# First loads on one queue in order of need, and the second group's patch products spread out, in a fusion block with routed experts

## The reference

```python
tokens = jnp.einsum('bpi,hi->bph', patches, W) + b
h = concatenate([cls, tokens], 1) * pos_embed
h = concatenate([h, txt], 1)                       # 16 x 193 x 128

x = layernorm(h)                                   # attention, 8 heads of 16
qk = x @ Wqk + bqk
q, k = elu(qk[..., :c]) + 1, elu(qk[..., c:]) + 1
z = 1 / (einsum('bhnd,bhd->bhn', q, mean(k)) + 1e-6)
kv = einsum('bhnd,bhne->bhde', rope(k) * scale, x * scale)
out = einsum('bhnd,bhde->bhne', rope(q), kv) * z
h = h + out + depthwise_conv3(x)                   # the "taps"

x = layernorm(h)                                   # 8 experts, best 2 of each token, and a shared one
shared = (silu(x @ sw1) * (x @ sw3)) @ sw2
y_e = (silu(x @ w1[e]) * (x @ w3[e])) @ w2[e]
h = h + sum over the best two of p_e * y_e + shared
```

## Time and profile before

| | us |
|---|---|
| median of three runs | 264.31 |
| the profiled execution's own time | 264.31 |
| its span, first to last instruction | 262.5 |
| TensorE busy | 233.8 (89% of the span) |
| VectorE busy | 189.9 (72%) |
| ScalarE busy | 155.3 (59%) |
| GpSimd busy | 115.2 (44%) |
| moved by DMA | 31.68 MB |

### The profile page before, as it was taken

One profiled execution on the slowest core, in us unless ns is written; L12 is line 12 of the kernel. 1 busy time (PEld: TensorE's weight loads), 2 busy tenths in 40 slices (PEclk: granted clock), 3 DMA queues, 4 the chain that ended last, 5 costly groups with the idle time before them and its releaser, 6 DMA issues.

```text
span 262.5 us, 5589 instructions
## 1 busy us (share of the span) xinstructions
PE 233.8 (89%) x1491; PEld 192.2 (73%) x1491; DVE 189.9 (72%) x737; ACT 155.3 (59%) x436; POOL 115.2 (44%) x121
## 2 busy tenths in 40 slices
PE   0499799999999999989899957999999999999960
PEld 0477688888879797966566636888888888888640
DVE  1533998798989898987988767766666666665784
ACT  0325458585858585875974325666666666666571
POOL 1400000055646464640656720676666666676600
PEclk9999799999999999997999997999999999999996
DMA  6989964143434301010011412324323332348736
GB/s 199 318 271 338 333 241 149 39 122 126 117 127 121 136 21 44 20 40 2 31 42 50 135 43 52 93 62 113 85 82 91 85 98 75 99 112 236 202 99 181
DMA packets 31421, 31.68 MB, mean 121 GB/s; under 512 B 4322, under 2 KB 27403, under 8 KB 30496
## 3 DMA queue, kind: packets, MB, share of 16 engines
q1 hardware_dynamic: 25960, 23.95, 30.7%
q0 software_dynamic: 3392, 6.36, 7.4%
q10 hardware_dynamic: 2040, 1.04, 1.4%
HBM read 22.80 MB, written 9.03 MB: 121 GB/s over the span
## 4 chain that ended last, share of the span: by engine, by line
PE 80%; DVE 9%; ACT 5%; ACTq 3%; issue 2%; DVEq 0%
PE bank L1565 15%; PE bank L1281 12%; PE bank L1585 10%; PE bank L1296 5%; PE bank L1574 5%; PE bank L1488 3%; PE bank L1473 3%; PE bank L1476 3%; PE bank L1369 2%; PE bank L1556 2%; PE bank L1329 2%; PE bank L1373 2%; PE bank L1295 2%; PE bank L1327 2%; PE bank L1355 2%
## 5 line engine op out<-in xcount | busy, mean ns | idle before, releaser
L778 POOL DMA_INDIRECT xs_dram<-xd,pos_i x50 | 54.9, 1099 | 82.7 <-DVE pos_i L967 69.9
L789 POOL DMA_INDIRECT y_dram<-att,goal x56 | 56.4, 1007 | 37.7 <-ACT att L713 37.4
L1281 PE MATMUL bank<-wt,xp_both 128*128 128x128 f32 x288 | 38.6, 288 | 0.0
L1281 PEld LDWEIGHTS bank<-wt,xp_both 128*128 128x128 f32 x288 | 36.9, 201 | 1.4 <-issue 0.7
L699 ACT ACTIVATE att<-bank 128x256 f32<-128x256 f32 x56 | 21.5, 383 | 24.9 <-PE bank L1565 24.9
L1585 PE MATMUL bank<-w_sb,att 128*128 x224 | 34.5, 277 | 0.0
L1190 DVE CAST xsT_h<-bank 128x128 fp32r<-128x128 f32 x56 | 16.3, 292 | 24.9 <-PE bank L1556 24.9
L1585 PEld LDWEIGHTS bank<-w_sb,att 128*128 128x128 f32 x224 | 29.4, 191 | 0.3 <-issue 0.2
L1565 PE MATMUL bank<-xp_both,xsT_h 128*128 x56 | 27.3, 488 | 1.5 <-DVE xsT_l L1192 1.5
L1203 DVE TENSOR_TENSOR att<-att,bank 128x256 f32<-128x256 f32 x56 | 23.0, 411 | 1.6 <-ACT att L699 1.6
L1565 PE MATMUL bank<-xp_both,xsT_l 128*128 x56 | 22.6, 403 | 0.0
(11 more groups left out here) (201 smaller groups left out, 497.2 us busy)
## 6 DMA issues: line engine op xcount, KB each, us to landing
xp_both<-in_patches SPq DMA_DIRECT2D x7, 1152.0 KB, 5.2
xs_all<-xs_dram SPq DMA_DIRECT2D x56, 64.5 KB, 1.8
xd<-y_dram SPq DMA_DIRECT2D x8, 384.0 KB, 4.6
w<-in_w SPq DMA_DIRECT2D x2, 1024.0 KB, 9.7
y_dram<-att,goal POOLq DMA_INDIRECT x56, 2.3
xs_dram<-xd,pos_i POOLq DMA_INDIRECT x50
hrow<-in_txt SPq DMA_DIRECT2D x2, 384.0 KB, 10.4
out_tokens<-hrow SPq DMA_DIRECT2D x6, 128.0 KB, 1.9
```

The lines of the kernel that those rows point to most:

```text
L778: nc.gpsimd.indirect_dma_start(out=xs_dram[:, :], out_offset=bass.IndirectOffsetOnAxis(ap=pos_i[0:rows, j, k:k + 1], axis=0), in_=xd[0:row ...
L789: nc.gpsimd.indirect_dma_start(out=y_dram[:, :], out_offset=bass.IndirectOffsetOnAxis(ap=goal[u][:, 0:1].bitcast(I32), axis=0), in_=ys[u][ ...
L1281: M(ps[:, 0:D], xp[p][:, k, :], wt[:, k, :], start=(k == 0), stop=False)
```

## The change

All loads but those of the class tokens and of the bias move from ScalarE's queue to SyncE's, into this order: three chunks of weights and patches, the constants, the last chunk, the rest rows, first text, projection matrix, positions, taps, router's bias, second text, then group 1; the destinations follow the other texts. On TensorE the parts 0, 1 and 2 of group 0 stand ahead of the class group's turn, and part 3 behind it; the class projection writes bank 6 instead of bank 1 and comes after all of group 0's parts; `turn_rows(0)` and the whole projection of group 0 follow it without a part of group 1 between; the parts of group 1 then stand behind the class group's turns, behind `turn_queries(0)`, and two behind `turn_turned(0)`. Parts 0 to 2 of group 2 keep their places. All groups use bank 7. ScalarE's and VectorE's orders for group 0 are written out to match, VectorE's `text_stats(3)` to `(7)` are spread over more places, and the remaining texts' means come in two turns (groups 2 and 3, then 4 to 7 at i = 3). From i = 2 on TensorE's order is as before.

```diff
@@ SyncE
             for i, (a, b) in enumerate(FIRST):
+                if i == len(FIRST) - 1:
+                    sp.dma_start(cst[:], consts[:, :]).then_inc(s_cst, 16)
                 sp.dma_start(wt[:, a:b, :], w_of_block[:, a:b, :]).then_inc(first_loaded[i], 16)
                 sp.dma_start(xp[0][:, a:b, :], patches_of(0)[:, a:b, :]).then_inc(first_loaded[i], 16)
             sp.dma_start(wt_rest[:], w_tok[KB * P:IN_D + 1, :]).then_inc(s_wtok, 16)
             sp.wait_ge(ones_set, 2)
             sp.dma_start(xr[0][0:KR, :], patches[KB * P:IN_D, :]).then_inc(s_wtok, 16)
+            sp.dma_start(hrow[:, 1:3, :], txt[0:2].rearrange("b t d -> t b d")).then_inc(txt_loaded[0], 16)
+            sp.dma_start(wqk_sb[:], wqk[:, :]).then_inc(s_wqk, 16)
+            sp.dma_start(posb[:], pos[1:1 + P, :]).then_inc(s_pos, 16)
+            sp.dma_start(cols[:], small[:, :]).then_inc(s_cols, 16)
+            sp.dma_start(gateb_sb[:], gate_b[:, :].broadcast_to([P, E])).then_inc(s_cols, 16)
             sp.dma_start(hrow[:, 4:6, :], txt[2:4].rearrange("b t d -> t b d")).then_inc(txt_loaded[1], 16)
...
@@ ScalarE
             act.dma_start(cls_in[:, 1, :], pos[0:1, :].broadcast_to([B, D])).then_inc(s_cls, 16)
-            act.dma_start(cst[:], consts[:, :]).then_inc(s_cst, 16)
-            act.dma_start(wqk_sb[:], wqk[:, :]).then_inc(s_wqk, 16)
             act.dma_start(bq_in[:], bqk[:, :].broadcast_to([4, 2 * D])).then_inc(s_bq, 16)
-            act.dma_start(posb[:], pos[1:1 + P, :]).then_inc(s_pos, 16)
-            act.dma_start(hrow[:, 1:3, :], txt[0:2].rearrange("b t d -> t b d")).then_inc(txt_loaded[0], 16)
-            act.dma_start(cols[:], small[:, :]).then_inc(s_cols, 16)
-            act.dma_start(gateb_sb[:], gate_b[:, :].broadcast_to([P, E])).then_inc(s_cols, 16)
-            act.dma_start(dest_sb[:], dests[:, :]).then_inc(s_ids, 16)
...
+            rstd_texts(1, 0, 1)
+            norm_texts(0)
+            class_columns()
+            rstd1(0)
+            norm_patches(0)
+            columns1(0)
+            class_exps()
+
+            exps_most(0)
+            by_turns(0)
+            exps_rest(0)
+            class_queries()
+            act.wait_ge(s_cols, 32)
+            centre_tap(0)
+            queries(0)
+            rstd_texts(2, 1, 2)
+            norm_texts(1)
+            key_sums(0)
+            turned_queries(0)
+            rstd1(1)
+            norm_patches(1)
+            inverse_log(0)
+            inverse(0)
+            columns1(1)
...
@@ VectorE
             text_stats(0)
-            dve.wait_ge(cls_act, C_EX)
...
             mean_texts(1, 0, 1)
             dve.wait_ge(s_pos, 16)
             patch_rows(0)
             patch_stats(0)
+            mean1(0)
+            text_stats(1)
+            dve.wait_ge(cls_act, C_EX)
...
+                if i == 2:
+                    text_stats(7)
                 elu_most(i)
...
@@ TensorE
+            tokens(0, 0)
+            tokens(0, 1)
+            tokens(0, 2)
             pe.wait_ge(s_cst, 16)
             pe.wait_ge(cls_act, C_ROW)
             T(bank[6][:, 0:B], xcls[:], ident[0:B, 0:B]).then_inc(cls_pe, 1)
-            tokens(0, 0)
-            tokens(0, 1)
-            pe.wait_ge(small_set, 2)
+            tokens(0, 3)
+            pe.wait_ge(small_set, 4)
             pe.wait_ge(s_wqk, 16)
             pe.wait_ge(bq_done, 1)
             pe.wait_ge(cls_act, C_COL)
...
+            turn_rows(0)
+            project_most(0)
+            project_rest(0)
             pe.wait_ge(cls_dve, C_FT)
...
             tokens(1, 0)
-            turn_rows(0)
+            turn_queries(0)
             tokens(1, 1)
-            project_most(0)
-            project_rest(0)
+            sums(0)
+            turn_turned(0)
             tokens(1, 2)
             tokens(1, 3)
...
+            attend(0)
+            turn_rows(1)
+            tokens(2, 0)
+            project_most(1)
+            mixed_rows(0)
+            project_rest(1)
+            tokens(2, 1)
+            tokens(2, 2)
+            for i in range(2, G - 1):
+                tokens(i, 3)
...
```

More of the change, by code:

```diff
@@ L565, in _, with class_columns, class_exps, class_queries @@
             A(xcls[:], hrow[0:B, CLS, :], ACT.Identity, bias=nm1[0:B, CLS:J], scale=rs1[0:B, CLS:J]).then_inc(cls_act, 1)
[L566 to L572, removed]
+            def class_columns():
+                act.wait_ge(cls_pe, C_ROWT)
+                nc.scalar.copy(xclsT[:], bank[6][:, 0:B]).then_inc(cls_act, 1)
+                for i in range(2):
+                    nc.scalar.copy(xT[i][:, 0:2], bank[6][:, 0:2]).then_inc(cls_act, 1)
+            def class_exps():
+                act.wait_ge(cls_pe, C_QK)
+                A(ex_c[:], bank[6][0:B, P:P + 2 * D], ACT.Exp, bias=-1.0).then_inc(cls_act, 1)
+            def class_queries():
+                act.wait_ge(cls_pe, C_QKT)
+                for k in range(2):
+                    nc.scalar.copy(qq[:, k, 0, :], bank[6][:, 32:34]).then_inc(cls_act, 1)
+                nc.scalar.copy(kc[:], bank[6][:, 64:65]).then_inc(cls_act, 1)
             def round_w13(e):
@@ L577, in round_w13 @@
                 nc.scalar.copy(w13_h[:, part], w13_flat[:, part]).then_inc(wh_done, 1)
[L579 to L585, removed]
-                    inverse(i - 1)
[L587 to L606, removed]
-                if i >= 0:
-                    key_sums(i)
-                if i >= 1:
-                    scores(i - 1)
-                if i >= 0:
-                    turned_queries(i)
-                if i + 1 < G:
-                    columns1(i + 1)
@@ new lines, in _ @@
+            rstd1(1)
[3 more added lines that the diff above has]
+            columns1(1)
+            for i in range(1, G - 1):
+                if i > 1:
+                    inverse(i - 1)
+                exps_most(i)
+                by_turns(i)
+                exps_rest(i)
+                centre_tap(i)
+                rstd2(i - 1)
+                if i == 1:
+                    rstd_texts(3, 2, 4)
+                if i == 3:
+                    rstd_texts(4, 4, G)
+                norm_texts(i + 1)
+                norm2(i - 1)
+                queries(i)
+                columns2(i - 1)
+                rstd1(i + 1)
+                norm_patches(i + 1)
+                key_sums(i)
+                scores(i - 1)
+                turned_queries(i)
+                columns1(i + 1)
@@ L831, in patch_rows @@
                 dve.wait_ge(tok_done, g + 1)
[L832 removed]
+                V.tensor_tensor(hrow[:, 3 * g, :], bank[7][:, 0:D], posb[:], ALU.mult).then_inc(hp_done, 1)
             def patch_stats(g):
@@ L1001, in _ @@
             patch_stats(0)
+            mean1(0)
+            text_stats(1)
+            dve.wait_ge(cls_act, C_EX)
+            V.scalar_tensor_tensor(out=ft_c[:], in0=ex_c[:], scalar=1.0, in1=bank[6][0:B, P:P + 2 * D],
+                                   op0=ALU.min, op1=ALU.max).then_inc(cls_dve, 1)
+            dve.wait_ge(turns_set, 6)
+            dve.wait_ge(small_set, 4)
+            elu_most(0)
+            elu_rest(0)
+            turn_parts(0)
+            turn(0)
+            dve.wait_ge(s_cols, 32)
+            tap_before(0)
             dve.wait_ge(cls_pe, C_KV)
             V.tensor_tensor(kv_c[:], bank[5][:, 0:D], mask, ALU.mult).then_inc(cls_dve, 1)
-            mean1(0)
-            text_stats(1)
-            dve.wait_ge(turns_set, 6)
-            dve.wait_ge(s_cols, 32)
+            mean_texts(2, 1, 2)
+            text_stats(2)
             dve.wait_ge(cls_act, C_SET)
             dve.wait_ge(cls_dve, C_KVC)
-            dve.wait_ge(small_set, 4)
-            for i in range(G - 1):
-                if i >= 1:
+            heads(0)
+            tap_behind(0)
+            patch_rows(1)
+            patch_stats(1)
+            text_stats(3)
+            mean1(1)
+            text_stats(4)
+            attended(0)
+            mixed(0)
+            text_stats(5)
+            text_stats(6)
+            for i in range(1, G - 1):
+                if i > 1:
                     mean1(i)
@@ L1272, in tokens @@
                 first, end = ((0, 5), (5, 10), (10, 15), (15, KB + 1))[part]
-                ps = bank[3 if g == 1 else 7]
+                ps = bank[7]
                 if first == 0:
-                    after(pe, hp_done, 0 if g == 1 else g)
+                    after(pe, hp_done, g)
                     after(pe, x_loaded[p], 32 * (g // 2 + p))
```

67 lines of the change are left out of this document (19 added, 48 removed).

## The result

| | us | runs |
|---|---|---|
| before | 264.61 (263.71 to 265.39) | 6 |
| after | 267.81 (266.67 to 269.09) | 6 |
| ratio after : before | 1.0116, 95% interval 1.0084 to 1.0148 | |

The change makes the kernel 1.2% slower, by 3.2 us. The profiled execution took 268.01 us, its span is 266.2 us.

The account below looks back on a forecast made before the run. TensorE's products bound each step from group 2 on, so gains lay in the first 39 us. An earlier start worth 3.3 us minus 1.9 for slow clock gave 1.4 less than 264.31: 262.9 us, range 261.0 to 265.0.

Parts of the forecast that it names:

- Loads: Start: last patch chunk lands at 11 to 12.7, `tokens(0)` ends at 13.4 to 15, constants land at 10.1.
- The rival of loads that interleave anyway: Start: last chunk still lands at 13.7, `turn_rows(0)` at 18.2; about 0.8 us less, 263.5; chance 0.10.
- The path to `turn_rows(0)`: Constants, bias ladder, text statistics and class columns lead there: 7.6 us from ladder at 10.15, so 17.7 instead of 20.86.
- From Q to the end of `project_rest(1)`: Groups 0 and 1: 15.0 us instead of 14.55, handing back 0.45; 3.3 us of lead left at full clock.
- Q: End of the first projection, where ScalarE's exponential starts: 24.25 before, forecast 20.45 at full clock.
- The clock: Idle TensorE before `turn_rows(0)` puts it and most of the first projection at 1.2 GHz: 1.3 to 2.4 us, taken 1.9.
- "no gain" rival: Slow clock lasts into group 1's patch products, 3.2 us instead of 1.9, constants later: about 264.4 us; chance 0.18.
- Cover of the rest: Moved loads, `text_stats(7)`, third `rstd_texts` and `mean_texts`, one PSUM bank: nothing, or 0 to 0.1 us in step 3.
- Group 1's loads: On SyncE: issued near 12.3, landed at 17.5, wanted by `tokens(1, 0)` at 22; free, 4 us to spare.
- Steps of 13.1 us: Loop over groups, from group 2 on: TensorE still bounds each step, which stays 13.1 us long.
- full clock: Rival: slow spell falls into the idle stretch before `turn_rows(0)`, costing nothing; 3.3 us less, 261.0; chance 0.15.
- Slower: Rival: constants land last, at 12.9, ladder and all behind 2.8 us later; 265.7 us, deciding from 11.5; chance 0.12.

Follow-up runs that it names:

- experiment 2: Kernel before with the new loads alone: 264.24 us, ratio 0.997; changed kernel with the old loads alone (orders alone): 266.93 us, ratio 1.01.
- experiment 1: Changed kernel plus 12 unread products in TensorE's pause before the class projection and 2 behind `turn_rows(0)`: 261.86 us, ratio 0.9893.
- experiment 5: Kernel before plus 5 unread products in its 1.38 us stall before `sums(0)`: 262.74 us, ratio 0.9914; repeated 262.93 us. Kernel before also profiled again: 266.31 us.
- experiment 3: Changed kernel with `project_most(1)` ahead of `tokens(2, 0)` again: 267.94 us, ratio 1.0111; experiment 1 with group 2 cut at 3, 8, 13: 263.14 us, ratio 0.9929.
- experiment 7: Changed kernel with constants' wait later in the bias ladder, 5 unread products, groups 1 and 2 recut, group 1's parts spread under waits: 261.7 us, ratio 0.9886.
- experiment 4: Changed kernel plus 5 unread products before the class projection, none behind `turn_rows(0)`: 286.12 us in a slow batch, ratio 1.0152.
- experiment 6: Changed kernel with constants' wait behind the bias ladder's first five operations, plus 5 and 2 unread products around `turn_rows(0)`: 262.0 us, ratio 0.9874.
- experiment 8: Six and four unread products where the experts start: on experiment 1 261.83 us, ratio 0.9885; on experiment 7 259.8 us, ratio 0.9801.

## Why the prediction was wrong

Forecast were 262.9 us (261.0 to 265.0) and a gain; it is 267.8 and a loss. By the prediction's own steps:

- **Loads.** `cosx` started at 10.25 (10.1 was said), `tokens(0)` ended at 13.8 (13.4 to 15). Right. The rival of loads that interleave anyway (`tokens(0)` at 16.1) did not happen, but the order of need is worth little: with the same orders and both queues `tokens(0)` ended at 14.7 (experiment 2), 0.9 later. The Trainium skill, "DMA: Bandwidth & Descriptors", "Issuing engines are not separate DMA queues", says that transfers started by several engines run on the same DMA engines and interleave. The loads alone agree, with no difference in time that can be told: ratio 0.997 (0.9938 to 1.0002).
- **The path to `turn_rows(0)`.** 17.88 was measured, 7.6 us behind the ladder's start as summed, and 17.7 said. Right.
- **From Q to the end of `project_rest(1)`.** 15.0 us at full clock were summed. Experiment 1, at full clock, has 35.70 - 20.45 = 15.25. Right, with the new stall before `turn_rows(1)` at 0.58 in the changed kernel (0.6 said). One reading in it was wrong without harm: the kernel before did not lose 1.6 us to its spell. Without the spell a wait of 1.35 stands in its place (experiment 5), and the sum has its own 0.6 for that wait.
- **The clock.** This is the step that failed. I saw that TensorE would be idle ahead of `turn_rows(0)`, said that the projection would run at 1.2 GHz, and took 1.9 us for it: 3.4 to 5 us of half rate. The length came from the single spell in the one profile. It was 13.7 us, from 18.4 to 32.1, with `turn_rows(0)` itself still at full clock ahead of it, and cost 5.7 us: 23.8 us from `turn_rows(0)` to the end of `project_rest(1)`, against 18.1 in experiment 1. Experiment 5 shows that even the kernel before, in another execution, had 10.2 us where that row has 3.4, and paid 4.0 us for it. The term was a draw from a wide spread, and I carried it as a measurement, also into the range: my "no gain" rival went to 3.2 us, and its own reason (the slow clock lasts into group 1's products) was the right mechanism, too short.
- **Cover of the rest.** One term is missing. The text ahead of the prediction says that parts 0 to 2 of group 2 keep their places. They don't: part 0 moved ahead of `project_most(1)`, as the diff shows, and with less work behind the projection a stall of 0.79 appears before `turn_second(0)` (experiment 3).
- **Group 1's loads.** Issued at 9.91, not 12.3, so the spare was larger than said: the second text stood on SyncE before too, and the six moved issues take 0.43 to 0.47 us each. Right in effect.
- **Steps of 13.1 us.** Right: `attend(1)` to `attend(3)` start at 49.76, 62.92 and 76.22. The step of 13.30 is the third, where 0 to 0.1 was said for the third `rstd_texts` and `mean_texts`; the kernel before has 13.16 there.

With the two corrections the sum closes. Full clock was 261.0; the stall makes it 261.8, and experiment 1 has 261.86. The clock's 5.7 on top, and the 0.3 by which `turn_rows(0)` is later than in experiment 1, make 267.8, and the changed kernel has 267.81. That it closes so well is in part luck. The profile of the kernel before has a later spell that the sum leaves out, in a window:

```profile
118.50:121.80 3.30, 3.30 (x8) 1.95 (x8) 2.56 (x9) 0.72 (x3) 0.00 (x0) 0.50 0.00 0
```

From `attend(6)` to `attend(7)` that profile takes 11.98 us, and those of the changed kernel and of experiment 1 take 10.94 and 10.95. From there to the end it takes 138.7 us, and they take 139.5 and 139.1. The two differences nearly cancel.

Of the rivals, "full clock" is what the orders are worth if TensorE is kept busy, but for the stall of 0.8. "Slower" was given 0.12 for a mechanism that did not happen: the constants landed at 10.2, below the 11.5 from which it decides. A loss through the clock, the one that came, had no chance of its own.

## What to carry to other kernels

An order that starts work earlier also makes holes, and a hole ahead of dense products can cost more than its own length: 3.07 us of idle time here were followed by 13.7 us at half rate. Before moving TensorE's work forward, ask what it does while the next input is on its way. Products that nobody reads are a cheap cover (14 of them turned +1.2% into -1.1%), though too many of them delay what they cover (experiments 1 and 7), and a real part of a later group, cut to fit the hole, is as good if its data are there. Take the price of a pause from several executions, and look at the granted clock of each: the worst one seen is what the range must hold, not only the one that a single profile happens to show.

## What was not expected of the hardware

- A spell outlasts its cause by far, and TensorE's being busy does not end it at once: 13.13 us busy of 13.70 at 0.50 in the changed kernel, 6.80 of 6.80 in experiments 2 and 4. The first 40 us of the kernel before had 3.4 us of it in one execution and 10.2 in another. Lengths seen near the start are 3.4, 6.8, 10.2 and 13.7 us.
- Spells also came behind short stalls: 0.95, 0.44 and 0.57 us within 3.3 us (experiment 2, orders alone), or a single 0.80 or 0.78 (experiments 6 and 8). Others of the same length had none behind them, such as the 0.79 of experiment 1, or 1.10 and 0.57 within 4.1 us in experiment 7. What decides between them stays open.
- The Trainium skill, "TensorE: Matmul & The Clock Gate", Part 1, calls the cost of slow products at the start below 1% of a typical kernel's span and varying from run to run. The start agrees here: the first 20 products of the kernel before took 4.57 us in one execution and 3.94 in the other (experiment 5), 2.3 and 1.7 more than twice the later 1.12, under 0.9% of the span. The loss of this change is another one, a spell behind a pause at 14 us: 5.7 of 268 us are 2.1%.
- In one batch every kernel took some 7% longer, 284.74 against 264.66 us for the kernel before. Both batches are recorded with the same chip number, so another chip is not shown to be the reason. The slowness was not even: in that batch's profile of experiment 5's kernel `attend(0)` to `attend(2)` start at 31.64, 44.56 and 57.73, with the usual steps, and `attend(3)` only at 74.22. In all four profiles of the batch the chain has later stretches, of 0.7 to 4.2 us, that are put down to another core or an unknown queue. No run here explains it.
